# Attention and mixture-of-experts layer on one core: two-tile against four-tile look-ahead in the shared expert, with routing, table and bias add rearranged

## The reference, cut to what matters

```
x  = x + attention(layernorm(x)) @ OUT_w.T + OUT_b          # causal, 8 heads; called x1 below
xn = layernorm(x1)
scores = sigmoid(xn @ gate_w.T)                              # [T, 8]
top_scores, top_idx = top_k(scores, 2)
combine = 2.5 * top_scores / sum(top_scores)
shared  = silu(xn @ sw1) * (xn @ sw3) @ sw2
routed  = sum over the two chosen e of combine_e * (silu(xn @ w1[e]) * (xn @ w3[e]) @ w2[e])
out = x1 + shared + routed
```

## Time and profile before

| | us |
|---|---|
| median of 3 runs | 1486.96 |
| lowest, highest | 1484.05, 1494.01 |
| the profiled execution | 1488.37 |
| its span, first to last instruction | 1486.5 |
| mean granted TensorE clock | 0.969 |

### The profile page before, as it was taken

One profiled execution on the slowest core, in us unless ns is written; L12 is line 12 of the kernel. 1 busy time (PEld: TensorE's weight loads), 2 busy tenths in 40 slices (PEclk: granted clock), 3 DMA queues, 4 the chain that ended last, 5 costly groups with the idle time before them and its releaser, 6 DMA issues.

```text
span 1486.5 us, 22931 instructions
## 1 busy us (share of the span) xinstructions
PE 1377.3 (93%) x5750; PEld 671.1 (45%) x5751; DVE 951.4 (64%) x2758; ACT 890.7 (60%) x2587; POOL 452.0 (30%) x431
## 2 busy tenths in 40 slices
PE   6997999999999999899899977599999999999996
PEld 4553233333333332355455543255555555555553
DVE  3898998888888874588879885333344444444331
ACT  4663456766666777556555645266666666666663
POOL 0000000000000000000112243677777777777771
PEclk9997899999999999999999998799999999999998
DMA  7775410040050000256577763144444344433442
GB/s 219 231 218 161 109 40 5 24 96 5 9 125 5 1 5 12 84 179 204 144 191 176 211 130 78 45 72 74 74 73 73 71 73 71 73 71 71 71 73 34
DMA packets 124858, 136.83 MB, mean 92 GB/s; under 512 B 37046, under 2 KB 86590, under 8 KB 124774
## 3 DMA queue, kind: packets, MB, share of 16 engines
q1 hardware_dynamic: 101350, 96.56, 24.5%
q0 software_dynamic: 21520, 37.84, 13.8%
q10 hardware_dynamic: 1904, 1.46, 0.4%
HBM read 87.03 MB, written 48.83 MB: 91 GB/s over the span
## 4 chain that ended last, share of the span: by engine, by line
PE 73%; DVE 14%; issue 5%; DMA 4%; ACT 3%; SPq 1%; ACTq 0%; POOL 0%; DVEq 0%; POOLq 0%
PE psum L1052 28%; PE psum L1063 15%; PE psum L975 9%; PE psum L957 7%; PE psum L939 6%; PE psum L889 4%; DVE arena L1242 3%; DVE psum L1240 2%; DMA xn_rows<-xg 1%; DMA attn_cur<-attn_rows 1%; DVE stats L1123 1%; PE psum L960 1%; PE psum L1036 1%; ACT arena L723 1%; PE psum L882 1%
## 5 line engine op out<-in xcount | busy, mean ns | idle before, releaser
L1052 PE MATMUL psum<-arena,xg_t 128*128 (+2 forms) x1648 | 515.5, 466 | 18.9 <-DVE xg_t L1212 18.9
L824 ACT COPY act_t<-act_q 32x96 f32<-32x96 f32 x1648 | 431.8, 262 | 153.2 <-DVE act_q L1333 132.6
L1052 PEld LDWEIGHTS psum<-arena,xg_t 128*128 128x128 f32 x1648 | 315.2, 193 | 220.1 <-issue 63.9
L795 ACT ACTIVATE arena<-psum 128x512 f32<-128x512 f32 (+3 forms) x640 | 303.1, 536 | 172.1 <-PE psum L960 84.6
L657 POOL DMA_INDIRECT table<-const,slot_i x64 | 63.0, 984 | 845.1 <-DVE slot_i L1435 748.6
L673 POOL DMA_INDIRECT xq<-xn_rows,quad_rows x284 | 271.5, 956 | 94.2 <-issue 86.6
L1063 PE MATMUL psum<-arena,act_t 128*128 (+3 forms) x618 | 285.7, 598 | 6.2 <-ACT act_t L824 6.2
L1242 DVE TENSOR_REDUCE arena<-psum 128x1 f32<-128x512 f32 x384 | 251.5, 685 | 41.4 <-PE psum L939 40.8
L939 PE MATMUL psum<-arena 96*128 96x512 bf16 (+3 forms) x640 | 219.5, 363 | 17.2 <-DVE arena L1240 9.2
L957 PE MATMUL psum<-arena 99*128 99x512 bf16 (+3 forms) x640 | 215.0, 353 | 1.6 <-ACT arena L795 0.4
L1323 DVE TENSOR_TENSOR act_sb<-psum,silu 128x352 f32<-128x352 f32 x103 | 53.9, 523 | 238.8 <-ACT silu L847 238.2
(11 more groups left out here) (137 smaller groups left out, 843.3 us busy)
## 6 DMA issues: line engine op xcount, KB each, us to landing
arena<-qk_parts SPq DMA_DIRECT2D x48, 256.0 KB, 6.0
arena<-in_w SPq DMA_DIRECT2D x16, 704.0 KB
arena<-in_x SPq DMA_DIRECT2D x32, 256.0 KB, 4.3
x<-in_x SPq DMA_DIRECT2D x32, 256.0 KB, 3.5
xn_rows<-xg SPq DMA_DIRECT2D x32, 256.0 KB, 2.6
xq<-xn_rows SPq DMA_DIRECT2D x128, 64.0 KB, 2.9
out_rows<-y_sb SPq DMA_DIRECT2D x32, 256.0 KB, 3.3
qk_parts<-arena SPq DMA_DIRECT2D x16, 384.0 KB, 3.2
```

The lines of the kernel that those rows point to most:

```text
L795: nc.scalar.activation(probs[:, at_b % PS, d * P:], psum[:, NA + at_b % NBK, 0:CH - d * P], ACT.Exp, scale=float(HD) ** -0.5).then_inc(s_e, 1)
L824: i = nc.scalar.copy(dst, src)
L1052: i = nc.tensor.matmul(psum[:, bank + k % 2, 0:w], xg_t[:, k % 2, c, :], rhs, start=c == 0, stop=c == DC - 1)
```

## The change

**Look-ahead.** In the shared stage PE and DVE run `front` four tiles ahead instead of two (LEAD = 4), with four xg_t buffers, seven x1 rows instead of six (three of them lie in the last expert's w2, whose load is later for that), and the heads in attention grow from three HT, two HF and one HX to five, four and three. **Last logits.** The logits of tiles 29 to 31 are no longer extra columns of `up`: `last_logits` computes them in twelve products of 8 columns within step 28, and the last two groups of two tiles become one of four, chosen at step 29. `block_list` runs at step 30. The ranks of a group come behind `up(n)` instead of ahead of step n. The first two `row_numbers` run within step 31, and the last two `store_y` follow the fourth block's table reads. **Bias.** POOL loads x again in sixteen pieces of 256 rows during attention, adds out_b, and stores the sum to xb_rows; `front` reads rows from there and no longer adds out_b. The first x1 rows are loaded at a later OT item. **Table.** A slot is 64 bytes wide instead of 8; a put still writes 8 bytes of it, a block's read fetches all of it (256 bytes for four slots instead of 32). The fill of the table is 2 MB instead of 0.27 MB and moves from projection into attention. **Down.** Its PSUM bank alternates between 5 and 6, in both expert stages. Group 2's puts no longer wait for steps of `up`.

```diff
-GROUPS = ((0, 8), (8, 8), (16, 8), (24, 4), (28, 2), (30, 2))
+GROUPS = ((0, 8), (8, 8), (16, 8), (24, 4), (28, 4))
+LEAD = 4
+AHEAD = 3
+SCORE_AT = {8: 0, 16: 1, 24: 2, 28: 3, 29: 4}
 CHOOSE = {9: ((0, 0),), 10: ((0, 1),), 11: ((0, 2),), 17: ((1, 0),), 18: ((1, 1),), 19: ((1, 2),),
-          25: ((2, 0),), 26: ((2, 1), (2, 2)), 28: ((3, 0), (3, 1), (3, 2)), 30: ((4, 0), (4, 1), (4, 2)), 31: ((5, 0), (5, 1))}
-COUNT_AT = {12: 0, 20: 1, 27: 2, 29: 3, 31: 4}
-PUT_AT = {0: 12, 1: 20, 2: 27}
+          25: ((2, 0),), 26: ((2, 1), (2, 2))}
+CHOOSE_FIRST = {28: 3, 29: 4}
+COUNT_AT = {12: 0, 20: 1, 27: 2, 28: 3, 29: 4}
+PUT_AT = {0: 12, 1: 20}
 TABLE = E * T + E * P
...
-    heads = [("HT", 0), ("HT", 1), ("HF", 0), ("HT", 2), ("HF", 1), ("HX", 0)]
-    for item, back in reversed(list(zip(heads, (9, 8, 7, 6, 5, 2)))):
-        plan.insert(last_b[-back] + 1, item)
+    heads = [("HT", 0, 10), ("HT", 1, 9), ("HF", 0, 9), ("HT", 2, 8), ("HF", 1, 7), ("HT", 3, 6), ("HF", 2, 6), ("HT", 4, 5),
+             ("HX", 0, 4), ("HX", 1, 3), ("HF", 3, 2), ("HX", 2, 1)]
+    for what, k, back in reversed(heads):
+        plan.insert(last_b[-back] + 1, (what, k))
...
+        xb_rows = dram("xb_rows", [T, D])
-        table = dram("table", [TABLE, 2])
+        table = dram("table", [TABLE, PAIR])
...
+        xb = [carve(2 * D).rearrange("p (t n) -> p t n", t=2) for _ in range(2)]
...
-        xg_t = sb("xg_t", [P, 2, DC, P])
+        xg_t = sb("xg_t", [P, LEAD, DC, P])
...
-        XR = 6
-        x1 = sb("x1", [P, XR, D])
+        XR = 7
+        x1_low = sb("x1", [P, XR - HC, D])
+        x1 = [x1_low[:, r, :] for r in range(XR - HC)] + [w2[:, E - 1, r, :] for r in range(HC)]
...
-                    if n == 2:
-                        for k in range(XR - 1):
-                            sp.dma_start(x1[:, k, :], rows(io["x"], k)).then_inc(s_xr[k], 16)
+                    if n == 1:
+                        spare = io["const"][:, CONST["spare_pairs"][0]:CONST["spare_pairs"][1]]
+                        blocks_of = table.rearrange("(b r) a -> b (r a)", r=P)
+                        for b in range(0, TABLE // P, P):
+                            m = min(P, TABLE // P - b)
+                            sp.dma_start(blocks_of[b:b + m, :], spare[0:m, :]).then_inc(s_table, 16)
...
+                    if n == NS - 5:
+                        for i in range(2):
+                            sp.wait_ge(s_xbs[i], 16 * NT // 4)
+                        for k in range(XR - 1):
+                            sp.dma_start(x1[k], rows(xb_rows, k)).then_inc(s_xr[k], 16)
...
-                if item == ("HT", 1):
-                    load_attn(2, 2)
-                if item == ("HF", 1):
-                    store_xn2(0, 0)
-                    load_quarters(0, 0)
+                if item[0] == "HT" and item[1] >= 1:
+                    load_attn(item[1] + 1, item[1] + 1)
+                if item[0] == "HF" and item[1] >= 1:
+                    store_xn2(item[1] - 1, item[1] - 1)
+                    load_quarters(item[1] - 1, item[1] - 1)
...
-                if k < NT - 4:
-                    load_attn(n + 4, k + 4)
-                if k < NT - 2:
-                    store_xn2(n + 2, k + 2)
+                if k < NT - LEAD - 2:
+                    load_attn(n + LEAD + 2, k + LEAD + 2)
+                if k < NT - LEAD:
+                    store_xn2(n + LEAD, k + LEAD)
                 load_expert(n // 4, n % 4)
-                if k < NT - 2:
-                    load_quarters(n + 2, k + 2)
-                if k >= 1:
+                if k < NT - LEAD:
+                    load_quarters(n + LEAD, k + LEAD)
+                if 1 <= k < NT - 1:
...
+                if k == NQ - 1:
+                    for t in (NT - 2, NT - 1):
+                        store_y(sh, io["out"], t, t)
...
+            x_pairs, xb_pairs = (a.rearrange("(n t p) d -> n p t d", t=2, p=P) for a in (io["x"], xb_rows))
+
+            def load_x_again(n):
+                if n >= 2:
+                    pool.wait_ge(s_xbs[n % 2], 16 * (n // 2))
+                pool.dma_start(xb[n % 2], x_pairs[n]).then_inc(s_xbl[n % 2], 16)
+
+            pool.wait_ge(s_vout, NCH)
+            pool.wait_ge(s_bv, 32)
+            load_x_again(0)
+            for n in range(NT // 2):
+                if n < NT // 2 - 1:
+                    load_x_again(n + 1)
+                pool.wait_ge(s_xbl[n % 2], 16 * (n // 2 + 1))
+                nc.gpsimd.tensor_tensor(xb[n % 2], xb[n % 2], out_b[:, :].rearrange("p (a n) -> p a n", a=1).broadcast_to([P, 2, D]),
+                                        ALU.add).then_inc(s_xba, 1)
+                pool.wait_ge(s_xba, n + 1)
+                pool.dma_start(xb_pairs[n], xb[n % 2]).then_inc(s_xbs[n % 2], 16)
...
-                            out=table[:, :], out_offset=bass.IndirectOffsetOnAxis(ap=slot_i[:, q, tt:tt + 1], axis=0),
+                            out=table.rearrange("r (s a) -> (r s) a", a=2), out_offset=bass.IndirectOffsetOnAxis(ap=slot_i[:, q, tt:tt + 1], axis=0),
...
+                    if ss is sh and n in SCORE_AT:
+                        scores_of(SCORE_AT[n])
                     if k >= 1:
                         move(n - 1, k - 1)
-                    if ss is sh and k < count - 3:
-                        to_copy(n + 3, k + 3)
-                    if ss is sh:
-                        for t0, m in GROUPS:
-                            if n == t0 + m:
-                                scores_of(t0, m)
+                    if ss is sh and k < count - LEAD - 1:
+                        to_copy(n + LEAD + 1, k + LEAD + 1)
...
-                    if k >= 1:
-                        pe.wait_ge(ss["ye"], n)
+                    if k >= 2:
+                        pe.wait_ge(ss["ye"], n - 1)
                     for c in range(HC):
                         r = P if c < HC - 1 else HL
                         rhs = sh2[0:r, c, :] if shared else w2[0:r, bass.ds(e, 1), c, :].rearrange("p a n -> p (a n)")
-                        i = nc.tensor.matmul(psum[:, 6, :], act_t[0:r, k % 2, c, :], rhs, start=c == 0, stop=c == HC - 1)
+                        i = nc.tensor.matmul(psum[:, 5 + k % 2, :], act_t[0:r, k % 2, c, :], rhs, start=c == 0, stop=c == HC - 1)
...
+                    if shared and k < count - LEAD:
+                        front(n + LEAD, k + LEAD)
+                    if shared and k < count - LEAD - 1:
+                        turn(n + LEAD + 1, k + LEAD + 1)
+                    up(n, k, expert(n))
                     if shared and n in COUNT_AT:
-                        ranks(COUNT_AT[n], min(n + 3, NT))
-                    if shared and k < count - 2:
-                        front(n + 2, k + 2)
-                    if shared and k < count - 3:
-                        turn(n + 3, k + 3)
-                    up(n, k, expert(n))
+                        ranks(COUNT_AT[n], min(n + LEAD + 2, NT))
+                    if shared and n == NT - AHEAD - 1:
+                        last_logits()
...
+            def last_logits():
+
+                pe.wait_ge(s_x1, NT)
+                pe.wait_ge(sh["xte"], NT)
+                for t in range(AHEAD):
+                    for c in range(DC):
+                        i = nc.tensor.matmul(psum[:, 7, t * E:(t + 1) * E], xg_t[:, (NT - AHEAD + t) % LEAD, c, :], sh13[:, c, H:H + E],
+                                             start=c == 0, stop=c == DC - 1)
+                i.then_inc(s_gate, 1)
...
-                link(nc.vector.tensor_tensor(row, row, out_b[:, :], ALU.add), s_fl, (N_NORM + 1) * n + 1)
-                norm_stats([row], s_fl, (N_NORM + 1) * n + 1)
+                norm_stats([row], s_fl, N_NORM * n)
...
+                def shared_step(n):
+                    if n < count - LEAD:
+                        front(n + LEAD, n + LEAD, 7)
+                    first = CHOOSE_FIRST.get(n)
+                    if first is not None:
+                        if n + LEAD - 1 < count:
+                            turn(n + LEAD - 1, n + LEAD - 1)
+                        for part in range(3):
+                            choose(first, part)
+                        slots(first)
+                    if n == NT - 2:
+                        block_list()
+                    gated(n, n)
+                    quarter_turn(n, n)
+                    if first is None and n + LEAD - 1 < count:
+                        turn(n + LEAD - 1, n + LEAD - 1)
+                    if first is None and n in COUNT_AT:
+                        slots(COUNT_AT[n])
+                    for g, part in CHOOSE.get(n, ()):
+                        choose(g, part)
+                    if n == NT - AHEAD - 1:
+                        dve.wait_ge(s_gate, 1)
+                        nc.vector.tensor_copy(logits[:, NT - AHEAD:, :], psum[:, 7, 0:AHEAD * E].rearrange("p (t e) -> p t e", e=E)).then_inc(s_lg, 1)
+                    if n == NT - 1:
+                        for k in range(2):
```

(23 more changed lines are left out.)

127 lines of the change are left out of this document (62 added, 65 removed).

## The result

The changed kernel takes **1467.07 us** (median of 4, 1466.07 to 1467.51) against 1489.08 (4 runs, 1484.05 to 1494.01) for the kernel before: ratio 0.9838, 95% interval 0.9813 to 0.9864, so 1.6% faster. The forecast was 1462, with a range of 1450 to 1475. The profiled execution of after took 1466.79 us, its span 1465.0, at a granted clock of 0.971.

The account below looks back on a forecast made before the run. PE fills the routed stage, so only 48 us of PE waits in the shared stage could be gained. 1488.4 - 25.8 + 1.5 = 1464.1 profiled; the median, 1.4 lower, is 1462.5, given as 1462, range 1450 to 1475.

Parts of the forecast that it names:

- main term: End of shared stage: POOL's last put ends at about 905.6 instead of 931.4, so the routed stage starts earlier: -25.8 us.
- the 1.5 for attention: Attention: small loads delayed once behind the bulk traffic of POOL's bias adds and the table fill, +1.5 us.
- the signs for being right: Trace signs, among them attn_cur waits under 3 us, 32 puts without gaps ending near 906, routed stage 507 us as before.
- The two waits: Heads in attention: PE waits for the first head's attention rows, +1.8 us, and for tile 4's, +2.5 us.
- new waits at the seam: Rival, attention's end or the seam: DVE's fronts and turns, or PE's end, cost 5 to 8 us each: 1472 to 1478; chance 0.12.
- a hold of DVE: Rival, attention: POOL's sixteen adds block DVE, growing attention 22 to 50 us, total about 1500 or 1493; chance 0.08.
- my bounds of 1.4 and 3.1: Attention: estimated time in us of one POOL bias add of 1024 columns, lower and upper.
- puts as dear in wide slots: Steps 12 to 27, upper bound: wide slots disturb transfers as before, so all 6.8 us of attention-row waits stay.
- no disturbance at all: Steps 12 to 27, lower bound: wide-slot puts disturb no other transfers, so attention-row waits fall from 6.8 us to 0.
- puts as dear as before: Rival, shared stage: the 6.8 us of attention-row waits stay whole, +3.4 us, total 1466; chance 0.20.
- 11 us of cover: End of shared stage: PE idle from its last down at 909 to routed data at 920.2, hiding block_list, last_logits and late selection.
- Everything hidden: Rival: wide puts disturb nothing, tile 4's head is not late, attention notices nothing: -7.4 us, total 1455; chance 0.15.

Follow-up runs that it names:

- half_puts: Changed kernel without the second choice's puts of tiles 16 to 31, so 16 of 32 late puts remain: 1457.14 us, ratio 0.9769.
- smaller_groups: Changed kernel with ranks and puts in groups of 8, 8, 4, 4, 4, 4 tiles, the third group in two halves: 1462.76 us, ratio 0.9783.
- after_again: The changed kernel unaltered, measured once more on another chip: 1466.70 us, ratio 0.9805.
- bias_timed: Changed kernel with GpSimd's bias adds one by one, each meant to wait for DVE's small chain on a chunk's maxima: 1464.03 us, ratio 0.9802.
- before_wide: Kernel before the change with only 64-byte table slots (and one constant made shorter): 1478.94 us, ratio 0.9909.
- combined: Changed kernel with timed GpSimd bias adds, moved heads, and groups of 8, 8, 4, 4, 4, 4: 1454.29 us, ratio 0.9713.

## Why the prediction was right

The main term held: the puts' queue set the start of the routed stage. From step 27's `up` to the last put's end I had 51.7 us and got 51.4 (858.10 to 909.47); from there to the routed stage 14.6 against 13.87. The 32 puts run at 1.27 us each as worked out from the earlier trace rows, and half_puts and smaller_groups show that their queue was the bound. The routed stage started at 923.34 where 920.2 and the 1.5 for attention gave 921.7; the routed stage itself took 541.6 us instead of 540.6; the time of the profiled execution is 1466.79 where I had 1464.1, the median 1467.07 where I had 1462. Two terms were mis-sized and partly offset one another, 7.4 us too little up to step 2 and 4.7 too much from there to step 27. That the sum came out within 3 us owes something to luck; a sign that I had named for being wrong, attention over 5 us longer with longer DVE operations, did come. Of the signs for being right, three missed: the first `up` at 633.70 (622 to 626), step 27 at 858.10 (850 to 857), and the wait of 7.76 us (9 to 13).

**The heads and attention: +2.2 at step 2 and +1.5 forecast, +11.1 measured** (638.13 to 649.19; +7.4 in after_again). The two waits were 1.91 and 1.51 us where I had 1.8 and 2.5. What I left out is the wait before the front product at 631.73, 2.76 us where the kernel before has 1.10: the rival "new waits at the seam" named DVE's fronts in the queue ahead of the last output items, and I judged that those wait for ACT. From the first attention load to the first `up` the heads cost 6.3 us (28.6 to 34.9) where I had 3.5, and up to step 2 2.9 to 4.4 where I had 2.2. The larger part is attention's own: the first attention load was 6.6 us late (4.5 in after_again). I had sized it by small loads behind bulk ones, +1.5, and excluded a hold of DVE because its large operations read PSUM. They were untouched. I had also misread the row that I took for the bound: in 210 to 240 us has PE at 27.91 us and DVE at 27.48, so DVE isn't the busier one there; it is in 126 to 200 us, where the loss stands (70.18 against 61.41). Between the large operations, on the path to the next maxima, DVE runs a chain of five operations of 128x16 in SBUF, and one of these is held for an add's length. The Trainium skill, "SBUF — State Buffer", SBUF: two separate sides, covers this: DVE operations with two SBUF inputs or in a 2-port mode share a pair of ports with GpSimd, and whichever instruction starts first keeps the other out for its whole length. The traces agree on the two-input ones (2.92 us in after and 2.90 in bias_timed for 0.17) and on the large ones from PSUM; the rule was applied to the long operations and not to the short ones on the chain. On the order they don't agree: in seven of the holds the DVE operation is recorded as starting 0.07 to 0.60 us ahead of the add, while POOL issued the DMA before it, and was held all the same. The rival's size was far off: one long hold and one of 0.65 us, not sixteen. Its 2.36 us an add lies between my bounds of 1.4 and 3.1. Its price was wrong by its own terms, too: sixteen blocks of 2.5 us less 24.3 make 1503, not 1493, and at 3.1 us 1512, not 1500.

**Steps 2 to 27: 213.6 forecast, 208.9 measured.** I had put 3.4 us of waits for attention rows and 1.3 for ranks; both were nil. The 3.4 was the middle between "puts as dear in wide slots" and "no disturbance at all"; the second is what before_wide shows, where PE has no wait for attention rows left, so the rival "puts as dear as before" falls. So does my reading of the Trainium skill, "DMA: Bandwidth & Descriptors", Specifications: that a transfer below 512 bytes is read, modified and written may hold, but it doesn't make the slot's width indifferent, since every put is of 8 bytes in both kernels and the stores' landings fell from 3.8 us in before to 2.2 in before_wide.

The end of the stage went as described, with other sizes: wait in `ranks` 3.98 us instead of 7 to 8, `last_logits` 5.27 instead of 2.4 to 3 (24 matmuls on the engine, not 12), the wait before the routed stage 7.76, under my 9 to 13, since PE's own end came 57.5 us after step 27's `up` and not 55, and the routed data a little sooner. PE's end, which I had as 11 us of cover, is thus the next bound, and of any repair there only some 6 us are gained, as half_puts shows. "Everything hidden", 1455, fell with the heads and attention; combined reaches that time, by 7.2 us from the groups and 2.6 from the heads in its trace.

## What to carry to other kernels

When work is moved to an idle engine, look at the shortest operations of the busy engine on its critical chain, too, not only at the longest: here those of 0.17 us were held, and those of 0.68 from PSUM were not. Small scattered writes are worth spacing out if other transfers are waited for beside them; the writer's own time won't show the difference. And when a queue of equal operations sets a stage's start, its length after the last input matters: split the groups so that less of it remains.

## What the runs showed of the hardware

- A DVE operation of 128x16 in SBUF, 0.17 to 0.18 us alone, was recorded for up to 3.0 us beside a GpSimd tensor_tensor of 128x1024 f32 (2.36 us). In eight of the executions there are thirteen of over 0.6 us, and each ended 0.04 us after the add. It happened to two-input operations and to a one-input TENSOR_SCALAR from f32 to bf16 alike; whether the latter ran in a 2-port mode, the trace doesn't say. A TENSOR_REDUCE of the same chain beside an add kept its 0.17 to 0.26 us.
- Beside puts of 8 bytes into slots 8 bytes apart, 256 KB stores took 3.8 us and 64 KB loads of attention rows 4.0 in the median (before, 700 to 900 us), with slots 64 bytes apart 2.2 and 2.9 (before_wide). In the changed kernel it was 2.8 and 3.4 with narrow slots, with single ones of 7.59 and 7.62. Which part of the memory path this is, stays open; no spacing between was tried.
- One kernel's executions spread by up to 10.6 us: smaller_groups took 1454.98 at a granted clock of 0.977 and 1465.54 at 0.965. Which of the two follows from the other, isn't shown. One profiled execution of each kernel is therefore read for the place of a wait, not for a difference of 2 us.
